# A decoder layer on one core: rounded values clipped by GpSimd instead of VectorE

## The reference, cut to what matters

```
xh = x @ H                                           # Hadamard matrix, 256 x 256
scale = clip(max(abs(xh), axis=-1), 1e-05) / 7
q = clip(round(xh / scale), -8, 7) * scale           # four bits
y = q @ ternary(weight).T
```

## Time and profile before

| | us |
|---|---|
| median of 3 runs (601.8 to 604.54) | 602.76 |
| the profiled execution | 602.27 |
| its span in the trace | 600.5 |
| TensorE busy | 528.7 (88%) |
| VectorE busy | 460.9 (77%) |
| ScalarE busy | 388.8 (65%) |
| GpSimd busy | 344.8 (57%) |

### The profile page before, as it was taken

The page is one execution under the profiler, slowest core; times in us unless marked ns, Lnnn a source line. Parts: engine busy times, 40 slices in busy tenths (PEclk is TensorE's granted clock), DMA queues, the critical chain, the costliest instruction groups (busy, mean ns, idle before and its releaser), DMA issues. The chain is left out here.

```text
span 600.5 us, 22290 instructions
## 1 busy us (share of the span) xinstructions
PE 528.7 (88%) x8180; PEld 451.2 (75%) x8180; DVE 460.9 (77%) x2867; ACT 388.8 (65%) x941; POOL 344.8 (57%) x336
## 2 busy tenths in 40 slices
PE   5577459999999989999999989998999999989941
PEld 3455337888778878887888878887888888878830
DVE  1777986868988997698889888989899998623213
ACT  2788765866667667675677657776686777555620
POOL 3458661975566646556375646665656556656831
PEclk9699757999999999999999999999999999999975
DMA  8253440010000010000100100010001000000000
GB/s 234 69 196 116 133 132 18 24 38 20 3 20 20 3 55 21 2 3 3 55 20 3 56 3 21 3 55 3 19 3 39 2 4 2 20 1 2 19 0 17
DMA packets 21932, 21.84 MB, mean 36 GB/s; under 512 B 1856, under 2 KB 19776, under 8 KB 21824
## 3 DMA queue, kind: packets, MB, share of 16 engines
q1 hardware_dynamic: 21824, 20.42, 10.9%
HBM read 18.32 MB, written 2.10 MB: 34 GB/s over the span
## 5 line engine op out<-in xcount | busy, mean ns | idle before, releaser
L484 POOL TENSOR_TENSOR h_lo<-h_raw,h_hi 128x512 f16<-128x512 f32 x128 | 149.1, 1167 | 126.5 <-ACT h_raw L607 125.4
L801 PE MATMUL ps_o<-w_hi,h_lo 128*128 128x256 f16 x512 | 139.8, 273 | 4.7 <-POOL h_lo L484 4.5
L785 PE MATMUL ps_z<-x1t_hi,w_lo 128*128 128x256 f16 x512 | 140.4, 274 | 0.7 <-DVE x1t_lo L951 0.7
L785 PE MATMUL ps_z<-x1t_lo,w_hi 128*128 128x256 f16 x512 | 140.1, 274 | 0.0
L785 PE MATMUL ps_z<-x1t_hi,w_hi 128*128 128x256 f16 x512 | 140.1, 274 | 0.0
L801 PE MATMUL ps_o<-w_lo,h_hi 128*128 128x256 f16 x512 | 139.6, 273 | 0.0
L801 PE MATMUL ps_o<-w_hi,h_hi 128*128 128x256 f16 x512 | 139.6, 273 | 0.0
L603 ACT ACTIVATE h_hi<-ps_z 128x512 f16<-128x512 f32 x128 | 76.0, 594 | 69.1 <-PE ps_z L785 69.1
L893 DVE MATCH_REPLACE8 taken<-next,taken 128x64 f32<-128x64 f32 (+4 forms) x480 | 110.5, 242 | 0.1
L505 POOL TENSOR_TENSOR acc<-go_sb,acc 128x512 f32<-128x512 f32 x56 | 71.4, 1274 | 58.2 <-ACT go_sb L617 57.4
L888 DVE MAX8 next<-taken 128x8 f32<-128x64 f32 (+4 forms) x480 | 85.3, 243 | 0.0
(11 more groups left out here) (118 smaller groups left out, 980.0 us busy)
## 6 DMA issues: line engine op xcount, KB each, us to landing
w_raw<-in_w1t SPq DMA_DIRECT2D x8, 512.0 KB, 4.3
w_raw<-in_w2t SPq DMA_DIRECT2D x8, 512.0 KB, 5.8
xt_sb<-in_xt SPq DMA_DIRECT2D x8, 256.0 KB, 3.4
x_sb<-in_x SPq DMA_DIRECT2D x8, 256.0 KB, 3.0
out<-out_sb SPq DMA_DIRECT2D x8, 256.0 KB, 2.2
xa_sb<-in_xt SPq DMA_DIRECT2D x7, 256.0 KB, 2.8
ctx_sb<-in_ctx_w SPq DMA_DIRECT2D x8, 128.0 KB, 3.0
itok_sb<-in_itok SPq DMA_DIRECT2D x8, 128.0 KB, 3.4
```

Of the source, the lines that this page charges most:

```text
L484: nc.gpsimd.tensor_tensor(h_lo[:, e % 2, 2 * z:2 * z + 2, :], h_raw[:, z, :, :], h_hi[:, e % 2, 2 * z:2 * z + 2, :], ALU.subtract)\
L785: last = pe.matmul(ps_z[z][:, d * UT:(d + 1) * UT], w[:, e, c, at:at + P], x[:, c, :], start=n == 0, stop=n == len(terms) - 1)
L801: last = pe.matmul(ps_o[e % 2][:, b * D:(b + 1) * D], h[:, e % 2, c, b * SEQ:(b + 1) * SEQ], w[:, e, c, :], start=n == 0, stop=n == len(te ...
```

## The change

The clip leaves VectorE's `quantise` and becomes a step of its own, `clip`, in GpSimd's queue: the same two operations (max, then min) on the same tile of 128 x 512 float32. It gets slots in all four tables. GpSimd waits for the third count of `quant_step`, ScalarE's `to_q4` waits for the new semaphore `clip_done`, and `quant_step` now counts three per unit. The last unit's `ffn_residual` moves from slot 78.5 to 90, behind the new step.

```
 STEADY:  "quantise": 82.5,  +"clip": 83.0,
 FIRST:   "quantise": 83.5,  +"clip": 84.0,
 SECOND:  "quantise": 82,    +"clip": 82.5,
 LAST:    "quantise": 85.25, +"clip": 85.75,   "ffn_residual": 78.5 -> 90
 UNIT_STEPS: ("dve", "quantise"), +("pool", "clip"), ("act", "to_q4"), ...
-            "hadamard": (quant_step, 4, lambda k: 3),
+            "hadamard": (quant_step, 3, lambda k: 3),
...
+                elif name == "clip":                      # GpSimd
+                    pool.wait_ge(quant_step, 3 * (v + 1))
+                    wait(pool, q4_ready, v)
+                    nc.gpsimd.tensor_scalar(clipped[:, :, :], rounded[:, :, :], ROUND - QNEG, ROUND + QPOS, ALU.max,
+                                            ALU.min).then_inc(clip_done, 1)
...
                 elif name == "to_q4":                     # ScalarE
-                    act.wait_ge(quant_step, 4 * (v + 1))
+                    act.wait_ge(clip_done, v + 1)
...
                     last.then_inc(quant_step, 1)          # VectorE, quantise
-                    dve.wait_ge(quant_step, 4 * v + 3)
-                    V.tensor_scalar(clipped[:, :, :], rounded[:, :, :], ROUND - QNEG, ROUND + QPOS, ALU.max,
-                                    ALU.min).then_inc(quant_step, 1)
```

More of the change, by code:

```diff
@@ L122 @@
     "turn_o": 36.5, "exp": 6.25, "copy_q4t": 84.5, "copy_k": -5.25, "x2t_high": 78.25, "normalise": 12.5,
-    "quantise": 83.5, "load_xt": 3.5, "store": 124, "gate_scale": 48.75, "x1t_low": 42.5, "x2t_low": 82,
+    "quantise": 83.5, "clip": 84.0, "load_xt": 3.5, "store": 124, "gate_scale": 48.75, "x1t_low": 42.5, "x2t_low": 82,
     "turn_q4": 86, "ln2_apply": 81.75, "ln2_stats": 76, "load_x": 20.25, "rstd2": 77, "copy_probs2": 9.75,
@@ L133 @@
     "turn_q4": 87.75, "normalise": 13.5, "ln3_apply": 107.25, "copy_q": -10.5, "copy_probs2": 10.25, "load_x": 19,
-    "gate_scale": 46.25, "rstd1": 36.75, "copy_v": 41.75, "gate_sums": 31.75, "quantise": 82, "load_xt": -10.5,
+    "gate_scale": 46.25, "rstd1": 36.75, "copy_v": 41.75, "gate_sums": 31.75, "quantise": 82, "clip": 82.5, "load_xt": -10.5,
     "gated_add": -1, "copy_k": -20.25, "to_q4": 84.75, "k": 19, "turn_probs2": 9,
@@ L139 @@
     "turn_probs2": 9, "shift1": 0.25, "copy_k": -11, "ffn": 94.75, "out_proj": 38.5, "attend": 13.5, "to_q4": 87.25,
-    "rstd2": 76.75, "copy_scores": -6, "ffn_residual": 78.5, "exp": 5, "ffn_scale": 88, "turn_o": 37.25,
+    "rstd2": 76.75, "copy_scores": -6, "ffn_residual": 90, "exp": 5, "ffn_scale": 88, "turn_o": 37.25,
     "turn_x2": 77.5, "copy_q4t": 89.25, "ln3_stats": 99.25, "copy_v": 32, "rstd1": 39.25, "store": 116.25,
-    "ln1_apply": 41, "ln2_apply": 76.75, "quantise": 85.25, "ln2_stats": 71.5, "v": 11.75, "load_xt": -11.75,
+    "ln1_apply": 41, "ln2_apply": 76.75, "quantise": 85.25, "clip": 85.75, "ln2_stats": 71.5, "v": 11.75, "load_xt": -11.75,
     "gate_scale": 49.75, "x2t_high": 82.5, "spread_q": -13.5, "rstd3": 98.75, "keep": 7.75, "copy_q": -12.25,
@@ L164 @@
     ("dve", "ln2_stats"), ("pool", "rstd2"), ("dve", "ln2_apply"), ("pe", "turn_x2"), ("act", "x2t_high"),
-    ("dve", "x2t_low"), ("pe", "hadamard"), ("dve", "quantise"), ("act", "to_q4"), ("pe", "turn_q4"),
+    ("dve", "x2t_low"), ("pe", "hadamard"), ("dve", "quantise"), ("pool", "clip"), ("act", "to_q4"), ("pe", "turn_q4"),
     ("act", "copy_q4t"), ("pe", "ffn"), ("dve", "ffn_scale"), ("pool", "ffn_residual"), ("dve", "ln3_stats"),
@@ L360, in decoder_layer @@
         s_zeroed = sem("s_zeroed")
-        quant_step, inv_ready, f_scaled = sem("quant_step"), sem("inv_ready"), sem("f_scaled")
+        quant_step, inv_ready, f_scaled, clip_done = sem("quant_step"), sem("inv_ready"), sem("f_scaled"), sem("clip_done")
         spread_ready, xb_ready, h_low_done = sem("spread_ready"), sem("xb_ready"), sem("h_low_done")
@@ L373, in decoder_layer @@
             "turn_x2": (x2t_low, 1, lambda k: 1),
-            "hadamard": (quant_step, 4, lambda k: 3), "turn_q4": (q4t_copied, 1, lambda k: 1),
+            "hadamard": (quant_step, 3, lambda k: 3), "turn_q4": (q4t_copied, 1, lambda k: 1),
             "ffn": (f_scaled, 1, lambda k: 1),
@@ L1001, in step @@
                         .then_inc(quant_step, 1)
-                    dve.wait_ge(quant_step, 4 * v + 1)
+                    dve.wait_ge(quant_step, 3 * v + 1)
                     V.tensor_scalar(xscale[:, :], amax[:, :], 1e-5, 1.0 / QPOS, ALU.max, ALU.mult)\
                         .then_inc(quant_step, 1)
-                    dve.wait_ge(quant_step, 4 * v + 2)
+                    dve.wait_ge(quant_step, 3 * v + 2)
                     V.reciprocal(xscale_inv[:, :], xscale[:, :]).then_inc(inv_ready, 1)
```

## The result

| | before | after |
|---|---|---|
| median, us | 603.35 (6 runs, 601.8 to 605.11) | 611.12 (6 runs, 609.17 to 611.84) |
| profiled execution, us | 602.27 | 610.29 |
| its span | 600.5 | 608.5 |

The ratio is 1.0123, 95% interval 1.0099 to 1.0147: 7.4 us slower, 6.0 to 8.9 (the two medians differ by 7.8, the means of the same runs by 7.4). Forecast were 2.2 us and a range up to 606.3. The sign was right, the size wrong by more than a factor of three.

A forecast was written before the change was run, and what follows sets the result against it. TensorE's almost gapless queue was taken to bound the body, a chain of waiting instructions the tail. Unit 0's 1.91 plus the tail's 0.29 made 2.20 us, on the median 602.76 giving 605.0; range 602.3 to 606.3.

The forecast's parts named there:

- The clip's price on GpSimd: Each 512-element clip on GpSimd takes 0.67 us, from a line through other tensor_scalar rows; bounds 0.56 and 1.26.
- Rival C: The clip costs GpSimd 1.26 us, like a two-input add; both exposed places grow by 0.59: 606.1 us; chance 0.15.
- The prediction's own sign of being wrong: Wrong if unit 0's `turn_q4` doesn't wait, the waits for `x` shrink, or the clip is over 1 us.
- Unit 0: The clip queues behind `h_low` on GpSimd, delaying `q` and TensorE's transposes by 1.91 us; bounds 0 and 2.50.
- The gaps of units 1 to 6: The clip fits GpSimd's gaps ahead of `h_low` and costs nothing; narrowest is unit 5's, 1.27 us.
- The tail: Unit 7's clip is fully exposed between `rounded` and `q`: 0.29 us later, bounds 0.18 and 0.88.
- VectorE's relief at nothing: Time freed on VectorE in the body gains nothing, since VectorE then waits longer for TensorE and ScalarE; bounds 0 and 6.07.
- Rival A: VectorE's relief shortens TensorE's waits for `x` in the body, gaining up to 6.07 us: 598.9 us; chance 0.08.
- B: Unit 0's delay is swallowed one unit later by the wait for `x`, 1.5 us at most: 603.5 us; chance 0.17.
- D: GpSimd's queue is held in every body unit, 1.91 us in each of seven: 616.4 us; chance 0.04.
- Why VectorE's clip took 0.43 to 1.2 us: Short clips in first and last unit have no GpSimd instruction beside them; others collide on the shared port pair.

The follow-up runs named there:

- unit 0 early: Changed kernel with unit 0's clip moved from slot 84.0 to 82.5, ahead of `h_low`: 605.27 against 603.46 us for the kernel before, ratio 1.0030.
- two mults: Changed kernel with two multiplications by 1 in place of max and min on GpSimd: 605.53 against 603.97 us for the kernel before, ratio 1.0036.
- no clip: Kernel before without the clip, ScalarE's `to_q4` reading `rounded` directly: 603.52 against 603.97 us, ratio 1.0000.
- the two with several forms: Two kernels with a different GpSimd tensor_scalar form in units' gaps, unit 0's clip placed early, part of unit 4 unclipped: 604.35 and 606.53 us, one execution each, not compared.
- unit 0 alone: Only unit 0 clips on GpSimd, the others on VectorE as before: 607.45 against 603.46 us, ratio 1.0071; repeated in one execution, 608.30 us.
- unit 7 alone: Only unit 7 clips on GpSimd, the others on VectorE as in the kernel before: 605.39 against 603.46 us, ratio 1.0030.
- units 1 to 6: Units 1 to 6 clip on GpSimd, units 0 and 7 on VectorE as in the kernel before: 603.49 against 603.97 us, ratio 0.9999.
- one mult: Only unit 0's clip on GpSimd, with one multiplication by 1 replacing max and min; others as before: 606.41 us, one execution.

## Why the prediction was wrong

- **The clip's price on GpSimd**: the step that failed. I put 0.67 with bounds 0.56 and 1.26; it is 1.92. The line through the earlier trace rows took "tensor_scalar with two operations" as one kind. The 1024-element row is two multiplications, one of the fast pairs (its line gives 667, measured 620). The upper bound was an add of two tiles and was not an upper bound for another operation; the 217 ns row, one addition on 2 elements, says nothing of the slope. Rival C had the right direction and a price 0.66 us short. The prediction's own sign of being wrong, "if the clip is over 1 us", is the one that came true.
- **Unit 0**: place and chain right. That 1.91 was forecast for a clip of 0.67 and 1.92 measured with 0.62 is closer than deserved: the chain let the clip start at the end of `h_low`, while GpSimd starts it 0.08 us later (185.43 + 1.16 to 186.67 there), which makes up for the 0.05. With 1.92 the same chain gives 1.91 + 1.25 = 3.16; measured 3.25 to the transposes (10.32 less 7.07 us behind the unit's first addition).
- **The clock**: not in the prediction, which booked a stall at its length. The stalls of 2.68 and 3.09 us cost 1.5 to 1.7 us on top, the one of 1.78 nothing. At the forecast price it doesn't matter, as the run with two multiplications shows; at my own upper bound of 1.26 the stall would lie between 1.78 and 2.68 us, where no run was made.
- **The gaps of units 1 to 6**: right at the forecast's price, and the narrowest named rightly (1.27 us). At 1.92 the clip sticks out of it and of unit 6's: 0.75 us. The widths of the gaps were read well; only the thing put into them was longer.
- **The tail**: 0.29 + 1.25 = 1.54, measured 1.58.
- **VectorE's relief at nothing**: right, by taking the clip away altogether. Rival A is out; B too, the delay of unit 0 is not swallowed (the stretches behind it give nothing back); D too, since units 1 to 4 lose nothing at their clips.
- **Why VectorE's clip took 0.43 to 1.2 us**: the prediction had the first unit's clip with no GpSimd instruction beside it. There is one: the clip runs from 176.45 to 176.88, and GpSimd's addition starts at 176.63. The clip started first and keeps its 0.43 us; the addition takes 1.36 instead of 1.27. In units 1 to 6 a GpSimd instruction was there first, and the clip took 0.78 to 1.2. Nothing of the sum hangs on it.
- Sum with the measured price, and the clock and the gaps as measured: 3.16 + 1.6 + 0.75 + 1.54 = 7.05, against 7.16 in the trace behind the first stretch. Of the 4.85 us beyond the forecast's 2.20, the price makes 2.50 at the two exposed places and 0.75 in the gaps, and the clock, which fell because the price made the stall longer, 1.6.

Open in part: the 0.24 us of the sixth stretch, 371.5 to 433.5 us. VectorE pauses there for 0.22 us, released by nothing that the profile shows ("issue"), in the selection of a tile; its `p_sb` comes late, and TensorE, which doesn't wait there in the kernel before, waits 0.39 us for it:

```profile
390.79 0.63 DVE L893 MAX8 next<-taken 128x8 f32<-128x96 f32 x3 [0.22 <-issue]
...
395.08 0.66 PE L753 MATMUL ps_pt<-ident,p_sb 128*128 128x128 f32 x4 [0.39 <-DVE p_sb L909]
```

All six traces with none of the eight clips on VectorE (this one, unit 0 early, two mults, no clip and the two with several forms) have the pause at this instruction and the longer stretch. The other six (before, unit 0 alone twice, unit 7 alone, units 1 to 6, one mult) have a pause of 0.27 to 0.29 us some 33 us later in the same stretch, ahead of `gate` or `rsum`, and lose nothing. So the 0.24 us comes with the clip's leaving VectorE's queue and not with GpSimd's clip; why the pause moves, no run shows.

## What to carry to other kernels

An operation moved to another engine has no price until a row shows that very pair of operations there; where none does, the nearest rows of other operations are no bounds, and the range must say so: here they gave 0.56 to 1.26 us and the clip took 1.92. In an order written by hand, look for the new step's queue neighbour: here it is `h_low`, which waits for ScalarE, while ScalarE's next step waits for the moved one. One slot number undoes it. And a stall of TensorE at full clock may have to be charged twice, for itself and for slow matmuls behind it: here stalls of 2.7 to 3.1 us cost some 1.6 us more.

## What the runs showed of the hardware

GpSimd's tensor_scalar at 512 float32 elements takes 0.62 us for mult with mult or add, 1.5 for mult or max alone, 1.92 to 1.94 for max with min (constants), add with add, mult with min: adding a multiplication by 1 to a single one makes it 0.9 us shorter. After a stall of 2.68 or 3.09 us, 12 to 15 expert matmuls ran at 1.2 GHz (0.21 us from start to start, against 0.11), after 1.78 us none. GpSimd's first additions of the units (`acc<-go_sb,x`) have a median of 1275 ns in the changed kernel and 1410 in the one before; there the five that start while VectorE's clip runs take 1.36 to 1.47 us, the other three 1.26 or 1.27.
